# Last batch's output jobs moved into feed-forward block 0 of a gated cross-attention and FFN kernel; its exponentials' logits over two bank pairs; block 0's input tiles in four buffers; expert chunks later

## The reference, cut to what matters

```python
# x: 16 batches x 256 rows x 512;  ctx: 16 x 256 x 256;  32 heads of 16
q = layernorm(x) @ Wq;  k, v = split(ctx @ Wkv)
q, k = rope(q, pos), rope(k, pos)
w = softmax(q @ k.T / 4)                       # per head, 256 x 256
x = x + tanh(g_xattn) * ((w @ v) @ Wout + bout)

h = layernorm(x)
logits = h @ gate_w                            # 8 experts, top 2
y = square(relu(h @ up_w)) @ down_w            # 512 -> 2048 -> 512
y = y + (h @ expert_weight) * sum(top2(logits))
out = x + tanh(g_ffn) * (layernorm(y) * ln_gamma + ln_beta)
```

## Time and profile before

| | us |
|---|---|
| median of 3 timed runs | 1682.34 |
| lowest and highest of them | 1681.07, 1688.51 |
| the profiled execution, its own time | 1675.71 |
| the profiled execution, its span | 1673.9 |

### The profile page before, as it was taken

How to read it: one execution, slowest core, us unless ns; L and a number is a source line. 1 busy time by engine, 2 the same in 40 slices (tenths; PEclk the granted TensorE clock), 3 DMA queues, 4 the chain that set the end, 5 groups by cost and what they waited for, 6 DMA issues and landing times.

```text
span 1673.9 us, 27912 instructions
## 1 busy us (share of the span) xinstructions
PE 1568.5 (94%) x9760; PEld 1162.4 (69%) x9760; DVE 974.7 (58%) x1448; ACT 639.5 (38%) x962; POOL 295.2 (18%) x370
## 2 busy tenths in 40 slices
PE   5688899999999999988799999999999999999997
PEld 4455666666666666655477787887878878788786
DVE  6667777877777777765464542634426344263524
ACT  3254545555555555556353222222222222222221
POOL 5221222212222222200100100201002020020202
PEclk9699999999999999989899999999999999999999
DMA  5967677666667777772251010101101011010001
GB/s 173 180 135 134 146 151 171 171 135 160 155 145 162 142 156 140 152 153 79 87 152 51 32 44 1 51 26 33 44 0 51 25 33 44 0 51 25 32 19 38
DMA packets 76357, 154.13 MB, mean 92 GB/s; under 512 B 13304, under 2 KB 26744, under 8 KB 76280
## 3 DMA queue, kind: packets, MB, share of 16 engines
q1 hardware_dynamic: 76280, 153.06, 39.1%
HBM read 101.50 MB, written 50.33 MB: 91 GB/s over the span
## 4 chain that ended last, share of the span: by engine, by line
PE 71%; DMA 10%; DVE 7%; SPq 5%; issue 4%; ACT 1%; POOL 1%; DVEq 0%; POOLq 0%; ACTq 0%
PE pP L976 14%; PE pA L1157 10%; PE pO L976 10%; PE pB L1157 10%; PE pT L976 9%; PE pO L1083 4%; PE pA L1059 4%; DMA stq<-mT 3%; SPq L509 3%; PE pM L976 3%; DMA stq<-qT_scratch 2%; DVE mneg L1354 2%; PE pB L1071 2%; DMA qT_scratch<-qT 2%; PE pT L983 1%
## 5 line engine op out<-in xcount | busy, mean ns | idle before, releaser
L1354 DVE TENSOR_REDUCE mneg<-pA 128x4 f32<-128x1024 f32 x250 | 305.7, 1223 | 166.3 <-PE pA L1059 164.1
L882 ACT ACTIVATE probs<-pB 128x1024 f32<-128x1024 f32 x256 | 262.6, 1026 | 296.7 <-PE pB L1071 289.0
L1454 DVE TENSOR_TENSOR relu<-relu 128x512 f32<-128x512 f32 x128 | 88.3, 690 | 263.9 <-ACT hid L934 263.8
L707 POOL TENSOR_SCALAR var_eps<-meanvar 128x1 f32<-128x1 f32 x96 | 34.7, 362 | 1078.8 <-DVE meanvar L1246 1078.8
L1157 PE MATMUL pA<-dn,hid 128*128 128x512 f32 x768 | 199.0, 394 | 2.7 <-DVE hid L1456 2.0
L1157 PE MATMUL pB<-dn,hid 128*128 128x512 f32 x768 | 196.1, 391 | 0.0
L976 PE MATMUL pP<-fT,up 128*128 128x512 f32 x768 | 190.1, 396 | 0.0
L976 PE MATMUL pO<-fT,up 128*128 128x512 f32 x768 | 187.8, 393 | 2.5 <-issue 2.5
L1157 PEld LDWEIGHTS pA<-dn,hid 128*128 128x128 f32 x768 | 142.9, 188 | 38.3 <-DVE hid L1456 7.0
L976 PEld LDWEIGHTS pO<-fT,up 128*128 128x128 f32 x768 | 144.5, 188 | 35.2 <-issue 3.3
L1157 PEld LDWEIGHTS pB<-dn,hid 128*128 128x128 f32 x768 | 144.2, 188 | 31.0
(11 more groups left out here) (177 smaller groups left out, 1965.0 us busy)
## 6 DMA issues: line engine op xcount, KB each, us to landing
stk<-kT_scratch SPq DMA_DIRECT2D x192, 128.0 KB, 5.4
stq<-qT_scratch SPq DMA_DIRECT2D x192, 128.0 KB, 6.9
kT_scratch<-kT SPq DMA_DIRECT2D x32, 512.0 KB, 3.6
qT_scratch<-qT SPq DMA_DIRECT2D x32, 512.0 KB, 3.6
xin<-x SPq DMA_DIRECT2D x32, 256.0 KB, 8.0
xres<-x SPq DMA_DIRECT2D x32, 256.0 KB, 10.2
x_scratch<-xres SPq DMA_DIRECT2D x32, 256.0 KB, 3.7
fx<-x_scratch SPq DMA_DIRECT2D x32, 256.0 KB, 2.7
```

Source lines behind the costliest of these rows:

```text
L707: nc.gpsimd.tensor_scalar_add(var_eps[:], meanvar[:, 1:2], EPS).then_inc(ve_made, 1)
L882: nc.scalar.activation(probs[:, s % 4, :, :, :].rearrange("p a b s -> p a (b s)"), pB[:, :, :], ACT.Exp).then_inc(exp_done, 1)
L1354: nc.vector.tensor_reduce(mneg[par][:, :, 2 * u:2 * u + 2].rearrange("p t q -> p q t"), psum[:, :, :].rearrange("p q (t k) -> p q t k", t= ...
L1454: nc.vector.tensor_tensor(r[:], r[:], r[:], ALU.mult).then_inc(sq_made, 1)
```

## The change

1. **The output jobs of batch 15 go into block 0.** PE, ACT, DVE and SP stop phase 1 after iteration 15 (POOL still does `iteration(16)`, its residual sums). PE does a10 ahead of `hidden` of m = 0, a01 behind it, then `routing`, a11; aT0 behind step 1, O0 in step 2, aT1 behind step 2, O1 in step 3. ACT's and DVE's shares go to the same steps, the two stores to SP's chunk groups 2 and 3.
2. **The wait for the stores** (`x1_out`) moves to step 5 on ACT and DVE, ahead of the first split of an expert chunk, and behind the chunk groups on SP. The scaling of gamma and beta (`scale_affine`) leaves the way from iteration 15 to block 0 and goes behind O1 in step 3; only the gate's split stays, behind a00.
3. **Second logits of batch 15 over two bank pairs.** From step 3 on the odd steps use pA. A `logits_b` then waits for the exponential of two steps before, not of the one before; step 3 itself waits for the last of the maxima.
4. **Block 0's tiles in four buffers**: `fx`, `fres0`, `fres1`, `relu0`. All four are loaded at once in `first_loads`, and SP's later waits for them go.
5. **Chunks.** The four expert chunks go two steps later (ex0 with m = 8, not 6). Six chunks, not eight, are split before block 0, so each `w_at(m)` is two chunks earlier in the list; SP's order of loading relative to m stays.

```diff
+def last_logits(b, s):
+    return isinstance(b, int) and b == B - 1 and s >= DELAY
...
+        first_fx = [fx, fres[0], fres[1], relu[0]]
...
-            if m >= 6 and m < 6 + KC:
-                ffn_chunks.append(("ex", m - 6))
+            if m >= 8 and m < 8 + KC:
+                ffn_chunks.append(("ex", m - 8))
...
-        split_at = {(B - 1, 6): 0, (B - 1, 9): 1, (B - 1, 12): 2, (B - 1, 15): 3,
-                    (B, 3): 4, (B, 5): 5, (B, 7): 6, (B, 9): 7}
-        ahead_w = len(split_at)
+        split_at = {(B - 1, 6): 0, (B - 1, 9): 1, (B - 1, 12): 2, (B - 1, 15): 3}
+        ahead_w = 6
...
-            for i in range(B - 2 - 2 * ahead, B + 1):
+            for i in range(B - 2 - 2 * ahead, B):
                 iteration(i, i)
...
@@ SP, first_loads @@
-                load_fx(0)
+                for u in range(UT):
+                    sp.dma_start(first_fx[u][:], x1_d[u]).then_inc(first_in[u], INC)
@@ SP, after phase 1 @@
-            for t in range(TT):
-                sp.wait_ge(x1_out[t], INC * B)
+            load_residual(B - 1)
+            for key in ffn_chunks[4:8]:
+                load_w(key)
@@ SP, block 0 @@
-                        for key in w_at(m):
+                        for key in ffn_chunks[8 + 3 * m:11 + 3 * m]:
                             load_w(key)
+                        if m in (2, 3):
+                            store_x1(B - 1, m - 2)
+                    for t in range(TT):
+                        sp.wait_ge(x1_out[t], INC * B)
@@ ACT, end of iteration 15 @@
+                    take_av(B - 1, GROUPS - 1)
                     act.wait_ge(f_small, 3 * INC)
                     nc.scalar.copy(gt_s[:, :, 0:NEXP], gt_raw[:]).then_inc(gt_hi, 1)
+                    for key in ffn_chunks[4:ahead_w]:
+                        split(key)
@@ ACT, block 0, behind relu and square of step m @@
+                        if m in (1, 2):
+                            job(f"aT{m - 1}", B, B)
+                        if m == 5:
+                            for t in range(TT):
+                                act.wait_ge(x1_out[t], INC * B)
@@ PE, logits_b @@
-                if some(STEPS * b + s):
-                    pe.wait_ge(exp_done, STEPS * b + s)
+                two = last_logits(b, s)
+                if two and s == DELAY:
+                    pe.wait_ge(max_done, STEPS * B)
+                elif some(STEPS * b + s):
+                    pe.wait_ge(exp_done, STEPS * b + s - (1 if two else 0))
+                psum = pA if two and s % 2 else pB
@@ PE, block 0 @@
+                    if first_block and m == 0:
+                        job("a10", B, B)
+                        pe.wait_ge(av_taken, GROUPS * B)
                     hidden(j, par, m, first_block)
+                    if first_block and m == 0:
+                        job("a01", B, B)
+                        pe.wait_ge(gt_lo, 1)
+                        pe.wait_ge(m_taken, total("M"))
                     if m == 0:
                         routing(j, par)
+                    if first_block and m == 0:
+                        job("a11", B, B)
                     if m == 2:
                         routing_turned(j)
+                    if first_block and m == 2:
+                        job("O0<", B, B)
+                        job("O0", B, B)
+                    if first_block and m == 3:
+                        job("O1", B, B)
                     if 1 <= m < MC - 1:
                         shared(j, (m - 1,), first_block)
+                    if first_block and m in (1, 2):
+                        job(f"aT{m - 1}", B, B)
@@ DVE, ahead of block 0 @@
+            job("a00", B - 1)
+            split_gate()
+            job("a10", B)
+            dve.wait_ge(av_done, GROUPS * B)
@@ DVE, block 0 @@
+                    if first_block and m == 0:
+                        job("a01", B)
+                        for key in ffn_chunks[4:ahead_w]:
+                            split(key)
...
+                        if m == 0:
+                            job("a11", B)
+                        if m == 2:
+                            job("O0", B)
+                        if m in (1, 2):
+                            job(f"aT{m - 1}", B)
+                        if m == 3:
+                            job("O1", B)
+                            scale_affine()
+                        if m == 5:
+                            for t in range(TT):
+                                dve.wait_ge(x1_out[t], INC * B)
```

More of the change, by code:

```diff
@@ L360, in flamingo_gated @@
         fx_in = sem("fx_in")
+        first_in = [sem(f"first_in{u}") for u in range(UT)]
         fxn_made = sem("fxn_made")
@@ L915, in _ @@
             phase1(act, iteration)
-            for t in range(TT):
-                act.wait_ge(x1_out[t], INC * B)
             def fblock(j, par, first_block=False, last=False):
```

65 lines of the change are left out of this document (26 added, 39 removed).

## The result

The changed kernel takes **1660.88 us** (median of 4 runs, 1657.85 to 1668.22), the kernel before 1682.03 (4 runs, 1681.07 to 1688.51): ratio 0.9884, interval 0.9852 to 0.9917. It is faster, as forecast, but by more: the predicted 1669.9 and the low end of the range, 1663, both lie above the 1660.88. The profiled execution took 1657.85 us with a span of 1656.1, where the kernel before had 1675.71 and 1673.9.

A forecast was written before the change was run, and what follows sets the result against it. PE, busy for 94% of the span, was taken to bound the kernel. Savings of 9.92 + 1.99 + 0.50 = 12.4 us off the median 1682.34 gave 1669.9 us, with 8 in 10 held by 1663 to 1679.

The forecast's parts named there:

- every cover of part 1: In block 0, other PE work was to hide each wait of the moved output jobs, with 0.4 to 3 us in hand.
- part 1: Between the last a10 and block 0: moving the output jobs into block 0 saves 9.92 us, low end 7.5.
- no new wait in block 0: Denies the rival that chunks come a step late twice in block 0, losing 5.7 us: 1675.6 us, chance 0.13.
- no low clock there: Denies the rival that block 0 starts with 17 us at clock 0.50, losing 8.5 us: 1678.4 us, chance 0.10.
- nothing slower: Denies the rival that block 0 runs at half clock for most of 42 us: about 1690.8 us, chance 0.05.
- the term of 8.74 us: PE's own work on a01, a11, aT0, aT1, O0 and O1, subtracted from the 18.66 us between a10 and block 0.
- 9.92: The gain in us from moving the output jobs into block 0 if every wait is covered, also taken as the high end.
- part 2: In block 0: the chunk change removes PE's two waits for hid_lo, saving 1.99 us, range 0 to 2.5.
- Part 3: In the last batch's attention: two bank pairs and four tile buffers save 0.50 us of 5.20, range -1.0 to 2.0.
- "Part 3 is wrong if logits of step 8 wait for a DMA": In the last batch's attention: a sign that the 0.50 us forecast for bank pairs and tile buffers fails.
- My allowance of 2 to 3 us for the measurement: Added on each side of the forecast for timing spread, giving 1663 to 1679 us for 8 in 10.

The follow-up runs named there:

- e5: The changed kernel with eight chunks split ahead of block 0 instead of six, stores waited for one step earlier; traced once, 117.86 us from a10 to block 1.
- e7: The changed kernel with eight chunks ahead, expert chunks early and stores waited for in step 3; traced once, 116.59 us from a10 to block 1.
- e6: The changed kernel with expert chunks two steps earlier again, six chunks still ahead; traced once, 114.09 us from a10 to block 1.
- e12_jobs_only: The changed kernel with last-batch logits in pB alone, one tile buffer and early expert chunks; 1655.50 us, ratio 0.9908 to the kernel before.
- e4: The changed kernel with block 0's four tiles loaded one after the other through the one buffer fx; 1660.04 us, ratio 0.9887.
- e9: The changed kernel with block 0's tiles 1, 2 and 3 normalised one, two and two steps earlier; traced once, 29.80 us from step 3 to a10.
- e1: The changed kernel run again with the same code; 1657.87 us against 1672.52 for the kernel before, ratio 0.9893.
- e2_jobs_back: The kernel before with two bank pairs, four tile buffers and later expert chunks, output jobs still ahead of block 0; 1671.89 us, ratio 0.9986.
- e15_scalings_late: The kernel before with the gamma and beta scalings behind phase 1 and the gate's split later in iteration 16; 1670.18 us, ratio 0.9979.
- e8_filler: The kernel before with 86 useless identity transposes in the waits between output jobs; traced once, 18.57 us from a10 to block 0.

## Why the prediction was wrong

**Right: the mechanism, and every cover of part 1.** There is no bracket from a10 to block 1. The first relu starts at 813.08, 1.0 us behind the end of the first `hidden`; the clock is 1.00; O0 and O1 are 3.06 and 2.95 us long. ACT takes aT1 from 830.01 on, its splits and the relu behind it, and nobody waits for them. SP stores at 832.39 and 838.91; the wait in step 5 costs PE nothing. None of the rivals came: no new wait in block 0, no low clock there, nothing slower.

**Wrong by 1.7 us: the term of 8.74 us, what PE has to do wherever it stands.** I summed durations of instructions that stood alone (4 x 0.66 + 2 x 3.05). In a dense stretch they overlap, and what counts is start to start: 0.35 to 0.36 us for each of a01, a11, aT0, aT1 (812.24 - 811.88 the first of them), 2.90 for O0 and 835.34 - 832.55 = 2.79 for O1, 7.11 us together. Part 1 is (831.07 - 811.75) - 0.56 - 7.11 = **11.65 us** in this trace, not 9.92. It is made of the 8.07 us of waits, 2.0 us of low clock (4.60 - 3.05 for O0 and 1.12 - 0.66 for aT0), and 1.6 us that isolated work loses because nothing overlaps it. That last piece was not in my sum, and 9.92, which I also took for the high end, was none.

**Wrong by another 2 us in the mean: one trace taken for the kernel.** The stretch has two forms, 19.3 and 23.3 us in two traces each, and the page I had showed the cheap one. With the mean of the four, part 1 is worth 21.31 - 0.56 - 7.11 = 13.6 us. The trace could have warned: the earlier trace rows has the scaling of beta at 1.48 us, and the line ahead of it, which I didn't show, has the equal scaling of gamma at 0.48. So the length depends on what falls beside it.

**Right in size: part 2.** Block 0 from its first product to the gate of block 1 took 127.88 - 19.32 = 108.56 us before and 114.08 - 0.56 - 7.11 = 106.41 now: 2.15 us, for a forecast of 1.99. The reason given (one split and not three ahead of the relu) is borne out by e5 and e7. The later expert chunks, which I had not priced, are worth nothing beside six chunks ahead (e6).

**Part 3: sign and place right, size too small.** 0.50 forecast, 0.9 us at full clock. The first tile waits 1.26 us, not 1.6, the third 1.70, not 1.5. What I missed stands in e12_jobs_only: the logits of step 13 wait 0.67 us for an exponential. In the first trace of before this wait isn't there, because the low clock of the earlier trace rows had made the work ahead of it longer; it was hidden by the loss beside it. The two pairs take it away. "Part 3 is wrong if logits of step 8 wait for a DMA" was a bad sign: they do (0.36 us), but the product behind them waits for the exponential anyhow, 0.36 + 0.54 = 0.90 us against 1.17 where the DMA is in time (e4, e9).

**The sum and the range.** 11.65 + 2.15 + 0.9 = 14.7 us with the cheap form, 16.7 in the mean, where 12.4 were forecast. Off the median of 1682.34 that I started from, the latter gives 1665.6, inside my range. The remaining 4.7 us to 1660.9 stand in no place that the change touches: the kernel before had 1672.52 in the later runs, 9.5 us less than in the first, and the changed kernel 1657.87, 3.0 less, with unchanged code. The ratio of the later runs, 0.9893, is 17.9 us of 1672.5, that of e12 15.4 us. My allowance of 2 to 3 us for the measurement was the last step that failed: three runs showed a spread of 7 us, the code ahead of the change alone spreads over 22. Whether the change does anything for those parts was asked with e1 (s3 at 781.84, later than three of the four of before): nothing supports it, and the means of s3 don't either. In the two traces of before on one chip, two thirds of the spread were low clock; what sets the clock, and what makes the rest, stays open. By the later ratio my starting point, 1682.34, would have given 1664.3, inside the range: that the result lay below 1663 is in part luck.

## What to carry to other kernels

When work moves from a stretch with waits into a dense one, price it start to start from dense rows, and count the gain as the whole old stretch less that: waits, low clock and the overlap that isolated work misses. Before a sum is made from a bracket, ask whether its length depends on what happens to run beside it (an operation with two lengths in the rows is the sign), and then take several executions. Count chunks split ahead by where the late one stands among its step's splits, not by how many there are.

## What the runs showed of the hardware

- **VectorE beside GpSimd.** The same scaling takes 0.48 or 1.49 us, the same gate split 0.18 or 1.25, a chunk split 0.69 or 1.74 (e2_jobs_back), the long ones each beside one of POOL's additions of 1.3 to 1.5 us. The divisions of e15_scalings_late, which read PSUM, ran beside such additions (807.55 and 809.23) at their usual 0.42.
- **TensorE's clock.** It falls among waits of 0.8 to 1.4 us (0.74 from a10 to block 0 in e15_scalings_late), and with one code O0 and O1 took 4.49 and 3.06 us in one execution and 5.49 and 4.61 in another. With PE kept busy in these waits it was 1.00 (e8_filler). It is also what moves the long stretch ahead of the change: 697.75 or 709.99 us of busy time for the same instructions. The Trainium skill, TensorE: Matmul & The Clock Gate, Part 1, says that activity releases the throttle; e8 and the joined stretch agree, don't. What decides how long the clock stays low isn't shown.
- **Overlap.** Four transposes with a recorded 0.60 to 0.66 us take 0.36 from start to start between other dense work, and 12 products of 3.0 take 2.8 to 2.9.
